# One GNN layer on one core: VectorE's subtraction for the second half of a block, taken from behind a chain of small operations into the middle of it

## What is computed

```python
def reference(x, src, dst, edge_attr_128, W1, b1, W2, b2, ln_gamma, ln_beta):   # 50000 nodes, 25000 edges, 128 features
    h = jnp.maximum(_layernorm(x, axis=-1), 0.0)
    agg = segment_sum(edge_attr_128, src, num_segments=50000)
    z = jnp.concatenate([h, agg], axis=-1)
    z = silu(z @ W1 + b1)            # W1 256 x 256
    z = z @ W2 + b2                  # W2 256 x 128
    z = (z - mean(z)) * rsqrt(var(z) + 1e-05) * ln_gamma + ln_beta
    return x + z + h
```

## Time and profile before

| | us |
|---|---|
| time, median of three runs | 780.91 (779.41 to 783.76) |
| the profiled execution, its own time | 779.33 |
| the profiled execution, from its first to its last instruction | 777.7 |
| TensorE busy | 719.1, 92% |
| VectorE busy | 706.2, 91% |
| ScalarE busy | 629.1, 81% |
| GpSimd busy | 488.9, 63% |

### The profile page before, as it was taken

How to read it: one execution, slowest core, us unless ns; L and a number is a source line. 1 busy time by engine, 2 the same in 40 slices (tenths; PEclk the granted TensorE clock), 3 DMA queues, 4 the chain that set the end, 5 groups by cost and what they waited for, 6 DMA issues and landing times.

```text
span 777.7 us, 15386 instructions
## 1 busy us (share of the span) xinstructions
PE 719.1 (92%) x4554; PEld 594.4 (76%) x4554; DVE 706.2 (91%) x2275; ACT 629.1 (81%) x2034; POOL 488.9 (63%) x414
## 2 busy tenths in 40 slices
PE   7999998789999999999999999999999999999994
PEld 3555546668888888888888888888888888888883
DVE  8999997889898989898989898989898989898988
ACT  7999975568878788788887887888878887878793
POOL 3000017567877777777787777777877777777730
PEclk9999999799999999999999999999999999999997
DMA  5000000123332323232323232323332323222112
GB/s 201 1 2 1 2 4 23 46 73 104 102 104 103 103 104 102 103 105 101 103 102 104 101 102 99 106 101 103 104 102 101 103 102 106 103 91 80 50 65 78
DMA packets 28265, 65.89 MB, mean 85 GB/s; under 512 B 8473, under 2 KB 10028, under 8 KB 28180
## 3 DMA queue, kind: packets, MB, share of 16 engines
q1 hardware_dynamic: 15604, 51.90, 18.0%
q0 software_dynamic: 12576, 12.99, 6.6%
HBM read 52.05 MB, written 25.60 MB: 100 GB/s over the span
## 4 chain that ended last, share of the span: by engine, by line
DVE 33%; issue 33%; PE 13%; another core or an unknown queue 13%; ACT 6%; DVEq 0%
DVE stat L823 9%; DVE T L1034 7%; PE y L657 4%; ACT hi L548 4%; DVE lo L1022 2%; PE za L652 2%; PE pre L652 2%; PE za L645 2%; PE pre L645 2%; DVE R L1029 1%; DVE var L863 1%; DVE R L1004 1%; DVE guess L867 1%; ACT hi L546 1%
## 5 line engine op out<-in xcount | busy, mean ns | idle before, releaser
L435 POOL DMA_INDIRECT G<-in_edge_attr_dram,slot_edge x388 | 478.6, 1234 | 152.6 <-issue 110.3
L740 PEld LDWEIGHTS y<-w2c,S 128*128 128x128 f32 (+1 forms) x1556 | 189.9, 193 | 10.8 <-issue 2.8
L740 PE MATMUL y<-w2c,S 128*128 128x128 f32 (+1 forms) x1556 | 191.1, 276 | 2.1 <-ACT S L555 2.1
L1022 DVE TENSOR_TENSOR lo<-za,hi 128x1024 fp32r<-128x1024 f32 (+1 forms) x98 | 119.0, 1214 | 60.0 <-ACT hi L548 53.4
L538 ACT ACTIVATE H<-X,shift,rstd 128x128 f32<-128x128 f32 x392 | 163.8, 513 | 2.9 <-DVE shift L882 2.4
L715 PE MATMUL pre<-hi,w1h 128*128 128x512 f32 (+1 forms) x392 | 163.4, 417 | 2.3 <-issue 1.2
L716 PE MATMUL pre<-hi,w1l 128*128 128x512 f32 (+1 forms) x392 | 154.8, 395 | 0.4 <-issue 0.4
L555 ACT ACTIVATE S<-pre,b1c 128x512 f32<-128x512 f32 (+1 forms) x196 | 128.5, 731 | 12.0 <-remote 8.7
L720 PE MATMUL pre<-lo,w1h 128*128 128x512 f32 (+1 forms) x392 | 123.2, 395 | 0.2
L546 ACT CAST hi<-za 128x512 fp32r<-128x512 f32 (+1 forms) x98 | 59.5, 607 | 71.0 <-remote 67.7
L701 PE MATMUL za<-HOT,G 128*128 128x128 f32 (+1 forms) x784 | 104.8, 277 | 1.8 <-issue 1.1
(11 more groups left out here) (154 smaller groups left out, 1005.5 us busy)
## 6 DMA issues: line engine op xcount, KB each, us to landing
X<-in_x_dram SPq DMA_DIRECT2D x48, 512.0 KB
out_dram<-R SPq DMA_DIRECT2D x48, 512.0 KB
G<-in_edge_attr_dram,slot_edge POOLq DMA_INDIRECT x388
X<-in_x_dram SPq DMA_DIRECT2D x1, 424.0 KB
out_dram<-R SPq DMA_DIRECT2D x2, 192.0 KB
w1f<-in_L_gnn_W_dram SPq DMA_DIRECT2D x1, 256.0 KB
w2f<-in_L_gnn_W_dram SPq DMA_DIRECT2D x1, 128.0 KB
srci<-in_src_dram SPq DMA_DIRECT2D x1, 85.8 KB
```

The lines of the kernel that those rows point to most:

```text
L435: nc.gpsimd.indirect_dma_start(G[b.j][:, t, :], None, source, bass.IndirectOffsetOnAxis(ap=slot_edge[:, bass.ds(b.number(TILES, t), 1)], a ...
L740: done = nc.tensor.matmul(places[t][0:r], S[c][:, m, t * r:(t + 1) * r], w2c[:, m, :], start=False, stop=True, skip_group_check=True)
L1022: nc.vector.tensor_tensor(out=lo[c][:, :, w], in0=za[:, :, w], in1=hi[c][:, :, w].bitcast(F32), op=ALU.subtract).then_inc(lo_done, 1)
```

## The change

```diff
     SMALLS = 11
+    LO_PLACE = 5
     LAST_SMALLS = 9
...
                     if place == 0 and b.plus(-1).exists(NB) and b.n > 2:
                         one_hots(b.plus(-1))
+                    if place == LO_PLACE and b.n > 4 and b.plus(-2).exists(NB):
+                        split_low(b.plus(-2), 1)
                     if 3 <= place < 3 + TILES and b.plus(1).exists(NB) and b.n > 3:
                         statistics(b.plus(1), place - 3)
...
             def step(b):
-                split_low(b, 1)
+                if b.n < 3:
+                    split_low(b, 1)
```

## The result

On the first chip, the changed kernel takes **853.2 us** (median; 851.0 to 857.8), the kernel before 780.2 (778.8 to 783.8). The ratio is 1.094, with an interval of 1.088 to 1.100. I had said 757.8, in a range of 745 to 790. The sign was wrong, and the time lies outside the range.

What follows compares the result with a forecast made beforehand. No engine alone bounds it; a circle of waits does: 7.33 + 1.36 + 3.05 + 1.11 = 12.85 us a block. An earlier turn saves 0.5 us over 43 blocks, 21.5: 779.33 - 21.5 = 757.8 us, range 745 to 790.

Steps and rivals of the forecast that it cites:

- the turn without a pause: TensorE's turn follows its products at once, 1.78 us behind their start instead of 2.56; at most 0.78 us gained per block.
- the uncovered wait: VectorE's first scaling, now next to the shift, waits for `powers_done`: 0.13 us per block, free while VectorE has idle time.
- the eighth gather's wait for the ninth link: GpSimd's eighth gather of the step waits for a link at most 1.13 us later; fits its 2.84 us slack, costs nothing.
- The fourth rival: `hi` comes too late for the subtraction's new place, despite 0.50 us of margin; ends near no change; 3 in 100.
- this piece: ScalarE's cast starts 2.42 us after the turn's transpositions end by their rows; cause unnamed, most of the uncertainty.
- the first rival: TensorE's signal to ScalarE's cast grows later once TensorE no longer pauses; 0.48 to 1.02 us per block, 800 to 823; 0.20.
- priced at nothing: GpSimd's gathers: one at most 1.13 us later, within 2.84 us slack, the first earlier; no cost.
- the second rival: Nothing moves: the cast is tied to something the subtraction doesn't touch; 779 us, give or take 2; 0.12 with `hi` too late.
- The upper bound: Most the earlier turn on TensorE can gain: 0.78 us per block, a block of 12.07 at which TensorE is full.
- The third rival: ScalarE's cast follows VectorE's scaling pass, 0.13 us later per block, 5.6 us in all: 785 us; chance 0.12.

Runs made afterwards that it cites:

- the held turn: Changed kernel with TensorE's turn of a first half also waiting for VectorE's first scaling operation of that step: 848.3 us, ratio 1.088 to the kernel before.
- the one hold: Changed kernel with the first three gathers of each first half held until that half's results are done: 849.2 us against 772.4 for the kernel before.

## Why the prediction was wrong

**What held.** The place of the subtraction, its start without a wait in steady blocks (454.18, behind a link at 454.11), the turn without a pause (1.78 us behind the start of the products, as computed, and in 25 of 35 blocks 7.91 us behind the first subtraction; in the other ten the slow rows take the gain back), the uncovered wait (the scaling starts 0.17 us behind the shift, 0.21 forecast) and the eighth gather's wait for the ninth link (0.61 us, hidden) are all as written. The fourth rival, `hi` too late, did not happen in the block shown; it happens at the end of the program, at 701.28.

**What failed, first step: the distance from the turn to the casts and the next subtraction.** The forecast carried 3.05 us to the cast and 1.11 to the subtraction over into the changed kernel, 4.16 in all, and on that rests all of its gain. It measured 6.41 on average: 4.79 + 1.10 in the block shown first, 3.13 + 3.51 in the one behind it. The prediction had marked this piece as odd, 2.42 us late and without a cause, and gave it "most of my uncertainty"; but the range was then made of cases in which that piece keeps its size, plus two rivals near 780. A piece that can't be explained can't be priced as a constant in a kernel whose every other piece is being moved.

**Second step: the first rival's size and its mechanism.** It named the right place and the right sign, "the signal grows later", but got 0.20, although block 46, the only precedent in the trace, pointed that way. Its time, 800 to 823, was too low: it took 0.48 to 1.02 us per block, and (853.9 - 779.3) / 43 = 1.73 was measured. Its sign, over 3.8 us from turn to cast, would have missed the blocks in which only the second cast is late. Its mechanism, TensorE no longer pausing, is refuted by the held turn: 848.3 us with a pause of 1.00.

**Third step: gathers "priced at nothing".** I weighed GpSimd by its slack, 2.84 us, and by its waits, and saw that its first gather would come earlier, but gave that no price. GpSimd is now idle longer than before, and yet the round runs through it: its fourth gather waits for the first half's subtraction, and the late signal comes 1.06 us behind the end of the eight gathers, 14.55 us from subtraction to subtraction. The runs on chip 5 show that the gathers are needed: without them no signal is late (725.3 and 726.0 us). Whether the gather at the results, which is no longer held up, is what makes the change cost 73 us is not shown; the one hold that ran on the first kind left the run of eight whole (849.2).

**And the bound.** "No engine is the bound by itself" was true of that trace and not of the program: without the late signals TensorE is full at 11.83 us a block, before and after. On the second kind there is nothing for the change to gain, which is why the second rival, "nothing moves", is nearly right there for a reason that it did not give (1.004 instead of 1.000). The upper bound that I gave, a block of 12.07 at which TensorE is full, is 0.24 us above the block of 11.83.

The third rival, a signal tied to VectorE's scaling pass, is refuted by the same timelines: before, the cast stood 3.28 us behind the start of the scaling (415.41 against 412.13), now 5.34 us behind it in one block (462.42 against 457.08) and 2.47 in the next (474.56 against 472.09).

**What stays open.** Why TensorE's signals come late on some chips when indirect DMAs are issued; what of them is needed, the instruction, the descriptors or the completion signals; why an earlier subtraction makes it 73 us worse, by the uncovered wait, by the gather at the results or by something else. One more possibility I can't exclude, that the recording itself takes part. The traces of the first kind are thinner: that of the kernel before holds 5,910 semaphore events and the changed one's 6,590, while the changed kernel's on chip 8 holds 11,402. On the page this is seen in the landing times, which are missing on the first kind (first the changed kernel there, then on chip 8, then the changed kernel without gathers on chip 5):

```profile
X<-in_x_dram SPq DMA_DIRECT2D x48, 512.0 KB
...
G<-in_edge_attr_dram,slot_edge POOLq DMA_INDIRECT x388
```

```profile
X<-in_x_dram SPq DMA_DIRECT2D x48, 512.0 KB, 3.4
...
G<-in_edge_attr_dram,slot_edge POOLq DMA_INDIRECT x388, 3.1
```

```profile
X<-in_x_dram SPq DMA_DIRECT2D x48, 512.0 KB, 3.3
```

Events are lost where signals are late, and on chip 5 the landing times come back when the gathers are gone. Without gathers there are fewer events to record in any case (5,237 for the changed kernel on chip 5), so the counts compare only kernels that have them. The Trainium skill (NOTIFIC — the notification-queue block, "7.1 Overflow: three behaviours, one of which stalls the engine") says that the block which writes such records holds back whoever feeds it rather than lose a record inside. By that page records could slow an engine; the thinner traces fit a record path in trouble, but no run here shows that it was the cause.

## What to carry to other kernels

Before a wait is priced, ask what ended it: a releaser that the trace can't name, behind a row that ended 2.4 us earlier, is no fixed cost, and a forecast that moves work around it should carry its growth as the first case, not as a remainder. An engine's slack does not take it out of the round: if its work starts on something that the round makes, and the round goes on only when that work has ended, its length counts in full, pauses too. Where engines wait although none is full, compare the length of a block with the busiest engine's work in it, and try the kernel on a second chip before tuning for the gap: here 58 us of the kernel before (780.2 against 721.9) are gone on another chip with the schedule as it is. And when an operation goes into a chain, look at the last pass of the loop, where its input comes late and the whole chain waits behind it.

## What the runs showed of the hardware that I had not expected

- The same program takes 772 to 782 us on two numbered chips (5, 13) and 721.8 to 721.9 on four (2, 6, 8, 15); taken together on one chip the runs of the kernel before agree to 0.5% on chip 13, 0.8% on chip 5 the later time and 0.1% on chips 6 and 8.
- With indirect DMAs on GpSimd, TensorE's signals on the first kind come up to 4.2 us behind their rows' ends (458.23, seen at 462.39) and then in a bunch, 0.07 to 0.10 us apart. Without the gathers, or on the second kind, they are within 0.02 us where their events are recorded.
- In four traces of the first kind (853.9, 848.5, 863.7 and 850.7 us) the last late cast starts about 1.05 us behind the end of a run of eight gathers in 32 of 35 blocks (0.93 to 1.16).
- A gather that starts while VectorE adds the results is held up: in the kernel before it ended 2.14 to 2.15 us behind the results' start, whether it began 0.08, 0.21, 0.88 or 0.98 us behind it. One that began 0.07 us ahead took 1.00.
- Whether the gathers' queue moves 12.99 MB or 0.80 MB makes no difference to that: 853.2 and 850.9 us, on two chips.
- A lower granted clock (0.963 in the changed kernel) and late signals are separate: with 0.989 the time was still 848.3 us.
